# Two graph layers with experts: the experts' rows added in DRAM by the scatter, and a turned end stage

## What is computed

```python
x2 = m @ W_gc + b_gc + (feats @ W_res + b_res)       # m: degree-scaled sum over edges
vals, idx = top_k(x2 @ Wg + bg, 2); gates = softmax(vals)
h2 = gelu(rows @ w1[e] + b1[e]) @ w2[e] + b2[e]      # per expert e, at most CAP = 1024 rows
y  = x2 + sum over the row's two experts of gate * h2
L1 = (y - mean(y, 0)) * rsqrt(var(y, 0) + 1e-5) * gamma + beta
out = layernorm(feats + L1)
```

## Time and profile before

| | us |
|---|---|
| runs, median | 2736.12 |
| profiled execution: span, first to last instruction | 2422.4 |
| what lies around the span (median less span) | 313.7 |
| last scatter issued to end of span (2244.1 to 2422.4) | 178.3 |
| blocks of experts (first scatter 1815.7, last 2244.1) | 428.4 |

### The profile page before, as it was taken

How to read it: one execution, slowest core, us unless ns; L and a number is a source line. 1 busy time by engine, 2 the same in 40 slices (tenths; PEclk the granted TensorE clock), 3 DMA queues, 4 the chain that set the end, 5 groups by cost and what they waited for, 6 DMA issues and landing times.

```text
span 2422.4 us, 50506 instructions
## 1 busy us (share of the span) xinstructions
PE 1978.3 (82%) x15238; PEld 1741.2 (72%) x15238; DVE 1451.4 (60%) x3750; ACT 409.5 (17%) x1197; POOL 1536.4 (63%) x1509
## 2 busy tenths in 40 slices
PE   2899999999997645999999999968628999999550
PEld 1788888888986534888889898857517778777240
DVE  6977777777874496566565655316723333333878
ACT  0211121212110243000000000004302222222030
POOL 5777776767777665777777777764754444444723
PEclk9999999999998887999999999969859999999675
DMA  5444343434436105333333333352128865668513
GB/s 170 121 125 118 118 121 115 122 100 121 123 94 203 38 20 165 112 114 107 112 109 104 106 107 105 105 185 60 48 71 265 250 196 158 189 206 264 171 43 106
DMA packets 219949, 312.93 MB, mean 129 GB/s; under 512 B 46946, under 2 KB 165017, under 8 KB 219788
## 3 DMA queue, kind: packets, MB, share of 16 engines
q0 software_dynamic: 61648, 155.25, 21.9%
q1 hardware_dynamic: 103148, 102.08, 13.0%
q10 hardware_dynamic: 54992, 53.49, 7.4%
HBM read 298.22 MB, written 57.83 MB: 147 GB/s over the span
## 4 chain that ended last, share of the span: by engine, by line
PE 49%; DVE 16%; issue 14%; DMA 8%; POOL 7%; DVEq 5%; SPq 1%; POOLq 0%; ACT 0%; ACTq 0%
PE bank L992 14%; PE bank L1022 13%; DMA acc<-x_scratch,acc 5%; POOL gath L670 4%; PE bank L1222 4%; PE bank L1213 4%; PE bank L1039 3%; DVE oh_lo L1354 3%; PE bank L1043 3%; PE bank L1114 2%; DVE codes L1376 2%; DVEq L1383 2%; PE bank L1056 2%; DVE oh_hi L1354 2%; DVEq L1407 2%
## 5 line engine op out<-in xcount | busy, mean ns | idle before, releaser
L670 POOL DMA_INDIRECT gath<-in_x_dram,idx_t x512 | 566.3, 1106 | 227.2 <-issue 129.6
L670 POOL DMA_INDIRECT gath<-h_scratch,idx_t x512 | 529.7, 1035 | 192.6 <-issue 139.8
L992 PE MATMUL bank<-onehot,gath 128*128 128x128 f32 x4096 | 522.0, 286 | 30.0 <-DMA gath<-h_scratch,idx_t 23.2
L1022 PE MATMUL bank<-Y,X 128*128 128x128 f32 x4312 | 534.6, 277 | 0.0
L1022 PEld LDWEIGHTS bank<-Y,X 128*128 128x128 f32 x4312 | 519.6, 193 | 15.4 <-issue 0.9
L992 PEld LDWEIGHTS bank<-onehot,gath 128*128 128x128 f32 x4096 | 494.8, 200 | 41.3 <-DMA gath<-h_scratch,idx_t 30.8
L1354 DVE TENSOR_TENSOR oh_lo<-iota_lo,lohi_t 128x512 bf16<-128x512 bf16 x392 | 268.4, 685 | 69.3 <-PE bank L1004 50.2
L1388 DVE TENSOR_TENSOR acc<-acc,bank 128x256 f32 x256 | 107.2, 419 | 282.3 <-issue 264.0
L763 POOL DMA_INDIRECT y_scratch<-acc x96 | 97.1, 1012 | 208.7 <-DVE acc L1755 203.1
L1039 PE MATMUL bank<-codes,oh_lo 128*128 128x400 bf16 x408 | 140.9, 346 | 107.4 <-DVE oh_hi L1354 48.0
L1222 PE MATMUL bank<-acc 128*128 128x256 f32 x768 | 198.7, 381 | 4.0 <-issue 3.8
(11 more groups left out here) (224 smaller groups left out, 2323.3 us busy)
## 6 DMA issues: line engine op xcount, KB each, us to landing
acc<-in_L_gnn_w_dram SPq DMA_DIRECT2D x101, 512.0 KB
acc<-in_L_gnn_w_dram ACTq DMA_DIRECT2D x96, 512.0 KB
y_scratch<-zero_s ACTq DMA_DIRECT2D x49, 256.0 KB
y_scratch<-bias_s SPq DMA_DIRECT2D x98, 128.0 KB
Y<-y_scratch SPq DMA_DIRECT2D x14, 896.0 KB, 12.9
acc<-in_L_gnn_b_dram ACTq DMA_DIRECT2D x96, 128.0 KB
gath<-in_x_dram,idx_t POOLq DMA_INDIRECT x512, 2.9
gath<-h_scratch,idx_t POOLq DMA_INDIRECT x512, 2.8
```

Of the source, the lines that this page charges most:

```text
L670: pool.indirect_dma_start(out=gath[:, half, k, :], out_offset=None, in_=table, in_offset=bass.IndirectOffsetOnAxis(ap=idx_t[:, TD + t:TD + ...
L992: last = pe.matmul(WINB[half][:, (q * DC + c) * WIN:(q * DC + c + 1) * WIN], gath[:, half, k, c * P:(c + 1) * P], onehot[:, half, k, :], s ...
L1022: last = pe.matmul(DB[w % 2][:, c * P:(c + 1) * P], X[:, h, c * P:(c + 1) * P], panel[:, w % 2, h, :], start=(h == 0), stop=(h == NT - 1))
```

## The change

Three parts.

1. **The scatter adds.** `y_scratch` has one row per node (and 128 rows for padding) and starts as a second copy of `x2`: SP stores each tile twice. The scatter adds onto it in DRAM (`compute_op=ALU.add`). The two choices of one node now meet in the same row, so POOL waits, ahead of each scatter, until the previous block's scatter has landed. Padding rows go to rows of their own. The zeroing in layer 0 is gone.
2. **The gate travels with the row.** A slot holds 8 bytes, number and gate. DVE makes the gates per group in routing (Exp by ACT, `odds_of`), and in the experts' stage multiplies b2 by the gate and applies it in the same operation that adds b2. `row_ids` is one operation, not three.
3. **A turned end stage.** `y_scratch` is loaded once (6.4 MB) straight into `Y`. PE turns the tiles, ACT copies them to `yT` (256 channels along partitions, 6250 nodes along the free side), DVE takes column statistics there, and ACT applies the batch norm as one affine operation with a scale and a shift per partition. PE adds `X` (times identity) and turns `yT` back on top of it in PSUM; DVE takes row statistics and ACT norms the rows from PSUM, in 13 groups of four tiles.

The diff, cut to its core:

```diff
-    YROWS = 2 * NT * P
+    YROWS = (NT + 1) * P
@@ sync
-                    sp.dma_start(x2_d[ds(P * i, P), :], ...).then_inc(x2_stored, 16)
+                    for d, stored in ((x2_d, x2_stored), (y_d, y_begun)):
+                        sp.dma_start(d[ds(P * i, P), :], ...).then_inc(stored, 16)
...
+            for g in range(NG7):
+                wait_count(sp, y_turned, 2 * (g - 1))
+                for first, n, rows, k in parts(range(SEVEN * g, SEVEN * (g + 1))):
+                    i = SEVEN * g + first
+                    sp.dma_start(Y[0:rows, i:i + n, :], tile_rows(y_d, P * i, n, rows)).then_inc(y_full[g % 2][k], 16)
@@ gpsimd, blocks(j)
                     gather_rows(blk + 3, 1 - b)
                     spaced_wait(pool, yo_ready, blk + 1)
+                    spaced_wait(pool, yo_stored[1 - b], 16 * (j + b))
                     pool.indirect_dma_start(
                         out=y_d, in_=yo_s[:, b, :], in_offset=None,
                         out_offset=bass.IndirectOffsetOnAxis(ap=bids_s[:, b:b + 1], axis=0),
-                        bounds_check=ASSIGN - 1, oob_is_err=False).then_inc(yo_stored[b], 16)
+                        compute_op=ALU.add).then_inc(yo_stored[b], 16)
@@ scalar
-                    act.dma_start(y_d[2 * P * st:2 * P * (st + 1), :]..., zero_s...).then_inc(y_cleared, 16)
...
+            for g in range(3):
+                affine(g)
+            row_roots(0)
+            for g in range(last_group + 1):
+                if g + 3 <= last_group:
+                    affine(g + 3)
+                if g < last_group:
+                    row_roots(g + 1)
+                norm_rows(g)
@@ tensor  (RING = 8 banks, NORM_BANKS = 2 units per group, AHEAD = 4)
+            def add_x(u):
+                i, n = bank_units[u]
+                if u < RING:
+                    pe.wait_ge(yT_kept, 2 * NG7)
+                else:
+                    pe.wait_ge(out_ready, (u - RING) // NORM_BANKS + 1)
+                pe.matmul(banks[u % RING][:, 0:n * D], ident[:, :], X[:, i:i + n, :]..., start=True, stop=False)
+            def add_y(u):
+                i, n = bank_units[u]
+                pe.wait_ge(affine_done, u // NORM_BANKS + 1)
+                ... 2 * n matmuls of 128 columns, yT turned back ...
+                last.then_inc(rows_summed, 1)
+            for u in range(AHEAD):
+                add_x(u)
+            for u in range(len(bank_units)):
+                if u + AHEAD < len(bank_units):
+                    add_x(u + AHEAD)
+                add_y(u)
@@ vector
-                    v.tensor_tensor(yo_s[:, b, :], banks[6 + b][:, 0:D], b2_s[:, b, :], ALU.add)
+                    v.scalar_tensor_tensor(yo_s[:, b, :], banks[6 + b][:, 0:D], gate, b2g_s[:, b, :],
+                                           ALU.mult, ALU.add).then_inc(yo_ready, 1)
...
+            row_stats(0)
+            for g in range(len(norm_groups)):
+                if g + 1 < len(norm_groups):
+                    row_stats(g + 1)
+                row_scales(g)
```

More of the change, by code:

```diff
@@ L905, in keep_x2, with odds_of, keep_route @@
                 stage_sums([i for i in ahead if not isinstance(i, int) or i < NT])
+            def odds_of(g, half):
+                spaced_wait(act, gap_ready, g + 1)
+                act.activation(odds[:, half, :], gap[:, half, :], ACT.Exp).then_inc(odds_ready, 1)
+            def keep_route(s, groups):
+                n = G * len(groups)
+                for q in range(0, n, 2):
+                    if q == 4 and not (isinstance(s, int) and s == 0):
+                        odds_of(2 * s - 1, 1)
+                    if q == G + 5:
+                        odds_of(2 * s, 0)
+                    keep_x2([2 * G * s + t for t in (q, q + 1) if t < n])
+                if len(groups) == 1:
+                    odds_of(2 * s, 0)
             act.wait_ge(sums_final, 2)
@@ new lines, in _, with affine @@
+            act.wait_ge(col_step, 1)
+            act.activation(root_c, root_c, ACT.Sqrt).then_inc(col_root, 1)
+            act.wait_ge(col_step, 2)
+            def affine(g):
+                i, n = norm_groups[g][0][0], sum(k for _, k in norm_groups[g])
+                for c in range(DC):
+                    t = yT[:, c, P * i:P * i + tokens(i, n)]
+                    last = act.activation(t, t, ACT.Identity, scale=scale_c[:, c:c + 1], bias=shift_c[:, c:c + 1])
+                last.then_inc(affine_done, 1)
@@ new lines, in row_roots, with norm_rows @@
+            def row_roots(g):
+                i, n = norm_groups[g][0][0], sum(k for _, k in norm_groups[g])
+                act.wait_ge(rows_known, g + 1)
+                act.activation(row_t[:, RSTD, i:i + n], row_t[:, VAR, i:i + n], ACT.Sqrt).then_inc(rows_rooted, 1)
+            def norm_rows(g):
+                act.wait_ge(norm_known, g + 1)
+                for i, n in norm_groups[g]:
+                    bank = banks[i // BANK_ROWS % RING]
+                    for k in range(n):
+                        last = act.activation(X[:, i + k, :], bank[:, k * D:(k + 1) * D], ACT.Identity,
+                                              scale=row_t[:, RSTD, i + k:i + k + 1],
+                                              bias=row_t[:, NMR, i + k:i + k + 1])
+                last.then_inc(out_ready, 1)
```

349 lines of the change are left out of this document (159 added, 190 removed).

## The result

The changed kernel takes 2754.34 us (median of 5 runs, 2749.48 to 2781.89); the kernel before, measured beside it, 2719.58 (5 runs, 2709.43 to 2750.27). The ratio is 1.0142, 95% interval 1.0096 to 1.0188: slower by 1.4%, which is less than the 2% from which a difference is called one here. In a later comparison it was 2832.08 against 2819.53, ratio 1.0049 (1.0005 to 1.0094).

A forecast was written before the change was run, and what follows sets the result against it. PE was taken to bound layer 0 and the experts, no engine throughout the end stage; 2422.4 + 2 + 75 - 35 = 2464.4 us of span, plus 313.7 around it, gave 2778 us, range 2680 to 2880.

The forecast's parts named there:

- plus the 313.7 around it: Whole kernel: 313.7 us lie around the profile's span and are added to the predicted span of 2464.4 us.
- Scatter's wait, +75 us: Experts: each scatter waits for the previous landing; +67 us in 64 blocks with new weights, +8 in 32 others.
- plain landing of 2.4 us: Experts: the last plain scatter landed within 2.4 us with no other traffic, taken as the landing time from below.
- 1 us added for the reading: Experts, 32 blocks without new weights: an adding scatter takes 1 us beyond 2.4 us, for reading rows from DRAM.
- End stage, -35 us: From the last scatter's start to the end: 143 us against 178.3, range -50 to +5.
- 98 for the last part: End stage, 13 groups from first affine to last norm: 93.5 us, or 98 with a part at half clock.
- Routing +2: Routing and the experts' start: small DVE operations and two more column loads cost about +2 us, range 0 to +5.
- Zeroing in layer 0: 0: Layer 0: removing the 49 zeroing DMAs (12.8 MB) from a stage that PE paces changes the time by 0.
- A: Experts: the scatter's wait is hidden, as an adding scatter lands in 3.15 us or less; 2706 us, chance 0.18.
- B: Experts: the accumulate paces all blocks, landings of 6.26 and 4.4 us cost +200; 2903 us, chance 0.2.
- C: End stage runs at PE's pace, 50.3 us in place of 98, -83 for the stage; 2730 us, chance 0.09.
- D: End stage: PE stays at the half clock in the last part, 142 us for 98; 2822 us, chance 0.08.

The follow-up runs named there:

- AHEAD 2: The changed kernel with the product with X put two banks ahead instead of four; 2705.85 us, ratio 0.9906 to the kernel before; at the first level 2432.85 us, 1.0009.

## Why the prediction was right and wrong

It said 2778 us, +42 us or 1.5% over the median, "same" as the likeliest class; the time is 2754.34, +34.8 us or 1.3 to 1.4% over the kernel before. The path was right: the scatter's wait costs more than the end stage gives. That the sum came within some 7 us is in part luck. Against the profile of the same level the terms are +13 ahead of the experts (forecast +2), +65.6 (+75) and -24.3 (-35), so their errors have different signs, and the one profile is 27.5 us over its median. At the first level, which the prediction's rows came from, the loss would be some 57 us (the estimate above). Term by term, against the second-level profile:

- **"plus the 313.7 around it" was wrong.** Around the span lie 1.8 us. The 300 us were the difference between a profile at the first level and runs at the second, inside the layers, routing and the experts. The step did no harm only because the sum was formed as a difference to the median. It did harm to the size of the experts' term: the pace before is 4.87 us at the level of the runs, not 4.51.
- **Scatter's wait, +75 us: right in mechanism, +65.6 measured.** Releaser, place and the late gathers came as said. The pace of 5.74 and 4.34 us (mean 5.27) was too low, 5.56 measured (5.99 and 4.70): quiet blocks land in 3.83 us, not 3.4, which gives the 4.67 us above in place of 4.34, and the others land later than the 4.8 us assumed. It was compared with a before that was too quick as well (4.5), so the two errors cancel in part; at the first level, where the rows belong, AHEAD 2 shows +96.5. The hand-over was put at 0.94 us and is 0.84.
- **The plain landing of 2.4 us was read from a nearly empty scatter.** Of that last block only five rows were written; the padding was dropped, as the queue from 2245.5 to 2246.5 us shows:

```profile
DMA packets 48, 0.01 MB, mean 6 GB/s; under 512 B 46, under 2 KB 47, under 8 KB 48
```

That it priced a full block rightly (2.44 us for 128 rows, in the kernel with plain scatters) was luck. And the 1 us added for the reading left out that POOL itself is busy 0.6 us longer with an adding scatter.

- **Why a landing is long** was put down to reading before writing. The rule of the Trainium skill that was weighed (Collectives: The Full Stack, "The bandwidth ceiling": an add needs two source reads) is not shown by this trace: the profile counts 291.62 MB read and 51.85 MB written both with the adding and without. What the trace does show is four times the data packets and POOL's longer instruction. The Trainium skill's fit of 2.0 us plus bytes over 436e3 (DMA: Bandwidth & Descriptors, "Anatomy of one DMA") gives 2.3 us for 128 KB, an estimate. The quiet plain scatter of 128 KB took 2.44 us, and a quiet adding one 3.83, 1.5 us more than the fit.
- **End stage, -35 us: -24.3 measured.** The alternation of PE with DVE and ACT was read rightly from the order of the rows; the pause was put at 4.4 us a group and is 4.35. What failed is "98 for the last part": it took full clock with a small addition for the group's 4.1 us of PE work, and it measured 6.07, since after each pause most of the burst's first half runs at 1.2 GHz. 2665.4 to the end is 114.7 us in place of 98 + 5. The first parts were near: 4.1 us to the first load (3.4), 32 for loading and turning (32), 3.4 for the coefficients (4.5).
- **Routing +2: +8 at the second level, 0 at the first.** **Zeroing in layer 0: 0**, nothing contradicts it; it can't be told within what layers vary from run to run.
- **Rivals.** A (wait hidden) fell: the scatter waits 87 times. B (6.5 us a block) fell: 5.56. C (end stage at PE's pace) fell as a forecast, but is what AHEAD 2 gives: 97.9 us, where C's 50.3 in place of 98 make 95 (its factors, 25 x 1.03 and 98 x 0.256, add up to 50.8). D was half true: half clock for about half of each burst.

## What to carry to other kernels

A DMA that must be ordered behind the one before it turns its latency into the loop's pace, whatever its engine's busy share says. Once two targets took turns, the adding itself cost 0.08 us a block at the second level, so here a second target helped more than a cheaper operation would have; it has a price of its own where the targets are read back (31 and 23 us in the end stage), and at the first level it left 42.9 us of loss in the experts. When a product is placed ahead into a ring of buffers, count whose release it asks for: one group less ahead gave 56 us here, some 35 of them from the pause itself and 22 from the lower clock behind it (estimate above). Before a landing is taken as a price, see how many bytes that DMA moved. And before a sum is made against a profile, compare its span with the runs: the 300 us between them were another level, not an overhead, and stages measured at one level must not be added to medians of the other.

## What was not expected of the hardware

- One program has two levels of time in different comparisons (2431.54, and 2719.58 to 2821.68 us), with nearly equal times of single instructions (279 and 282 ns); the end stage without indirect DMAs is the same at both (178.3 and 178.2 us), and so nearly is the experts' stage once it hangs on the chain of scatters (5.53, and 5.54 to 5.61 us a block).
- An indirect scatter of 128 rows of 1 KB that adds keeps POOL busy 1.58 us in place of 1.00, goes as 128 packets of 1 KB where a plain one has 32 of 4 KB, and lands in 3.6 to 3.9 us quiet where a plain one needs 2.44. The profile counts the same bytes read and written for both.
- After a pause of 4.35 us PE's burst is at the 1.2 GHz level for its first half or from its second product on, and back at 2.4 before its 6 us are over; with pauses of 0.85 us, one to every two groups, the 8.1 us shown stay at 2.4.
